# A decoder layer on one core: the same instructions, each engine's stages in another order

## The reference

```
# 1. attention, 16 heads of 8: q, k from a linear map joined with a 3-tap convolution; v linear
scores = einsum('bhqd,bhkd->bhqk', Q, K) / sqrt(8)
scores = scores * tau[..., None] + delta[:, :, None, :]   # tau, delta: conv, gelu, conv, sigmoid of x
out = linear(softmax(scores) @ V)
x = layernorm(x + out)
# 2. mLSTM, 4 heads of 32, q = x, k = v = ctx; ig, fg: gates, linear in q, k, v
log_D = cumsum(log_sigmoid(fg))[s] - cumsum(log_sigmoid(fg))[t] + ig[t]   # t <= s, else -inf
C = (q @ k.T / sqrt(32)) * exp(log_D - max_log_D)
h = C / (max(|C.sum(-1)|, exp(-max_log_D)) + eps) @ v;  x = layernorm(x + headnorm(h))
# 3. ffn: x and weight rounded to an FP6 grid in blocks of 32
x = layernorm(x + quantised(x) @ quantised(weight).T + bias)
```

## Time and profile before

| | us |
|---|---|
| median of 3 runs | 239.37 |
| the runs | 236.99, 239.37, 241.14 |
| the profiled execution | 238.0 |
| its span in the profile | 236.3 |
| PE busy | 208.4 (88%) |
| PE weight loads busy | 132.0 (56%) |
| DVE busy | 154.1 (65%) |
| ACT busy | 134.2 (57%) |
| POOL busy | 132.0 (56%) |
| mean granted clock of PE | 0.949 |

### The profile page before, as it was taken

How to read it: one execution, slowest core, us unless ns; L and a number is a source line. 1 busy time by engine, 2 the same in 40 slices (tenths; PEclk the granted TensorE clock), 3 DMA queues, 4 the chain that set the end, 5 groups by cost and what they waited for, 6 DMA issues and landing times. The chain is left out here.

```text
span 236.3 us, 5909 instructions
## 1 busy us (share of the span) xinstructions
PE 208.4 (88%) x2217; PEld 132.0 (56%) x2217; DVE 154.1 (65%) x354; ACT 134.2 (57%) x346; POOL 132.0 (56%) x239
## 2 busy tenths in 40 slices
PE   1799889699999999899888899789889969699895
PEld 1676454244566455566546567366648756276552
DVE  4587889959444553557647779966684475556871
ACT  2632867556854643673763768757776465515332
POOL 7994629691232192581695848862781757523520
PEclk9997999979999999999999999999997967899799
DMA  5822110000000000202002003003002003000001
GB/s 145 206 37 78 47 47 0 1 0 3 0 3 3 0 3 1 92 3 81 11 1 94 3 1 115 0 25 97 23 0 67 28 8 103 3 22 1 22 1 47
DMA packets 10220, 8.40 MB, mean 36 GB/s; under 512 B 1872, under 2 KB 9264, under 8 KB 10192
## 3 DMA queue, kind: packets, MB, share of 16 engines
q1 hardware_dynamic: 8816, 7.83, 11.2%
q0 software_dynamic: 512, 0.18, 0.7%
q10 hardware_dynamic: 864, 0.01, 0.2%
HBM read 6.94 MB, written 1.08 MB: 34 GB/s over the span
## 5 line engine op out<-in xcount | busy, mean ns | idle before, releaser
L996 DVE TENSOR_REDUCE nm<-score 128x8 f32<-128x1024 f32 x32 | 39.1, 1223 | 22.0 <-PE score L740 22.0
L511 ACT ACTIVATE prob<-score 128x1024 f32<-128x1024 f32 x32 | 32.6, 1021 | 21.2 <-PE score L755 21.0
L740 PE MATMUL score<-km,qf 32*128 32x512 f32 x128 | 35.0, 640 | 0.8 <-ACT prob L511 0.7
L750 PE MATMUL score<-qm,kf 32*128 32x512 f32 x128 | 35.0, 639 | 0.8 <-DVE nm L996 0.8
L775 PE MATMUL pvb<-ones 128*128 128x512 bf16 x80 | 23.5, 436 | 0.0
L359 POOL CAST nmx<-nm 128x16 bf16<-128x16 f32 x16 | 4.1, 254 | 30.4 <-DVE nm L996 30.4
L381 POOL TENSOR_TENSOR u<-u,maskb 128x1024 f32<-128x1024 f32 x7 | 16.5, 2358 | 7.2 <-DMA u<-gates_out 7.2
L768 PE MATMUL pvb<-prob,vz 128*32 128x128 f32 x512 | 17.4, 277 | 2.2 <-ACT prob L511 2.2
L859 PEld LDWEIGHTS qkb<-ctm,cc 128*128 128x128 f32 x128 | 15.3, 194 | 4.3 <-issue 2.2
L768 PE MATMUL pvb<-prob,ez 128*32 128x128 f32 x512 | 16.9, 273 | 0.0
L859 PE MATMUL qkb<-ctm,cc 128*128 128x33 f32 x128 | 15.7, 278 | 1.3 <-DVE cc L1069 0.8
(11 more groups left out here) (248 smaller groups left out, 485.8 us busy)
## 6 DMA issues: line engine op xcount, KB each, us to landing
u<-gates_out SPq DMA_DIRECT2D x7, 512.0 KB, 3.7
xt<-in_x_dram SPq DMA_DIRECT2D x4, 256.0 KB, 4.3
cin<-in_ctx_dram SPq DMA_DIRECT2D x4, 256.0 KB, 3.4
out_dram<-th SPq DMA_DIRECT2D x8, 128.0 KB, 1.9
ck<-in_L_attn_convk_w_dram SPq DMA_DIRECT2D x1, 192.0 KB, 3.6
cq<-in_L_attn_convq_w_dram SPq DMA_DIRECT2D x1, 192.0 KB, 3.9
pk<-in_L_attn_kproj_w_dram SPq DMA_DIRECT2D x1, 128.0 KB, 2.9
pq<-in_L_attn_qproj_w_dram SPq DMA_DIRECT2D x1, 128.0 KB, 3.4
```

The lines of the kernel that those rows point to most:

```text
L511: nc.scalar.activation(prob[:, n % 2, 2 * h:2 * h + 2, :].rearrange("p g s -> p (g s)"), sc[:, 1024 * h:1024 * (h + 1)], ACT.Exp, scale=0. ...
L740: ins = mm(sc[:, 512 * q:512 * (q + 1)], qf[r, n, :], km[r, n % (2 * CB)].rearrange("p j s -> p (j s)"), start=True, stop=True)
L750: mm(sc[:, 512 * q:512 * (q + 1)], kf[r, m, :], qm[r, m % (2 * CB)].rearrange("p j s -> p (j s)"), start=True, stop=False)
L996: nc.vector.tensor_reduce(nm[:, n % RING, 8 * h:8 * (h + 1)], sc[:, 1024 * h:1024 * (h + 1)].rearrange("p (h s) -> p h s", h=8), AX_X, ALU ...
```

## The change

The core of the diff, with the numbers of some stages:

```diff
-    "warm": (172, 173, 174, 177, 178, 180, 181, 184, 186, 188, 190, 191, 194, 196, 197, 198, 199, 200, 201, 204, 205, 206, 207, 208, 210, 211, 213, 214, 215, 216, 217, 218, 219, 220, 222, 223, 225, 226, 227, 228),
+    "warm": (172, 174, 175, 177, 178, 179, 180, 184, 187, 189, 190, 191, 195, 196, 197, 198, 199, 200, 201, 204, 205, 206, 207, 208, 210, 211, 212, 213, 215, 216, 217, 218, 219, 220, 221, 222, 224, 225, 227, 228),
-    "nGT": (73, 97, 102, 127, 148, 158, 170, 187), "qk": (83, 104, 114, 133, 157, 168, 189, 193),
-    "hst": (88, 108, 119, 142, 164, 175, 192, 203), "xdT": (116, 128, 135, 163, 179, 195, 209, 221),
+    "gT": (67, 80, 105, 120, 139, 154, 167, 186), "nGT": (71, 95, 107, 123, 149, 164, 170, 188),
+    "qk": (81, 108, 122, 131, 152, 169, 185, 193), "hst": (85, 114, 126, 141, 156, 173, 192, 203),
...
                 if due("x2l", t) is not None:
                     dve.wait_ge(rs2_done, LATE + 1)
                     dve.wait_ge(qa_done, LATE)
+                    dve.wait_ge(x2b_done, LATE)
```

More of the change, by code:

```diff
@@ L44 @@
 PLACES = {
[10 rows of a table removed]
-    "hst": (88, 108, 119, 142, 164, 175, 192, 203), "xdT": (116, 128, 135, 163, 179, 195, 209, 221),
-    "ffn": (117, 129, 137, 166, 182, 202, 212, 224),
-    "warm": (172, 173, 174, 177, 178, 180, 181, 184, 186, 188, 190, 191, 194, 196, 197, 198, 199, 200, 201, 204, 205, 206, 207, 208, 210, 211, 213, 214, 215, 216, 217, 218, 219, 220, 222, 223, 225, 226, 227, 228),
-    "vzero": (0,), "wab_o": (1,), "tapt": (2, 10, 15, 18, 24, 26, 33, 34), "wm_o": (3, 7),
-    "tapd": (4, 5, 17, 20, 27, 29, 36, 38), "ww_o": (6, 12), "wt_o": (8,), "wd": (9,), "fb": (11,), "bias": (13,),
@@ L60 @@
-    "ko": (14, 32, 56, 60), "wo_o": (16,), "qo": (19, 28, 35, 41), "wr_o": (21,), "qs": (22, 30, 39, 42),
-    "wg_o": (23,),
-    "max": (25, 31, 37, 40, 43, 45, 47, 48, 51, 53, 57, 59, 61, 63, 67, 69, 76, 79, 81, 84, 88, 95, 99, 106, 111, 113, 116, 126, 130, 132, 135, 140),
[7 rows of a table removed]
-    "x2l": (185,), "xdl": (187,), "outl": (189,), "xe": (0, 8, 9, 17), "idt": (1, 2, 12, 13, 24, 26, 37, 38),
-    "idd": (3, 4, 14, 19, 30, 31, 42, 46), "get": (5, 10, 16, 21, 28, 32, 41, 43),
-    "ged": (6, 7, 20, 23, 34, 35, 47, 49), "cxe": (11, 22, 48, 58), "th": (15, 25, 36, 50), "dt": (18, 29, 40, 52),
@@ L73 @@
-    "cme": (27, 33, 39, 45, 51, 56, 60, 63),
-    "nmTe": (44, 55, 62, 66, 73, 77, 82, 90, 99, 107, 118, 127, 140, 144, 152, 162), "edx": (53,),
-    "exps": (54, 57, 59, 61, 64, 67, 70, 72, 75, 76, 79, 83, 86, 91, 94, 98, 101, 105, 110, 113, 122, 124, 130, 135, 142, 145, 147, 151, 158, 160, 167, 168),
[6 rows of a table removed]
-    "mkk": (0, 1, 2, 3, 17, 18, 19, 23, 36, 37, 40, 41, 49, 51, 52, 53), "res": (4, 5, 6, 12),
-    "mkq": (7, 8, 10, 11, 14, 15, 20, 22, 38, 39, 42, 43, 57, 58, 59, 60), "gcb": (9, 13, 21, 24, 26, 27, 31, 32),
[3 rows of a table removed]
@@ L87 @@
-    "out": (75, 81, 85, 96, 102, 107, 110), "x2b": (109,), "spread": (0, 1, 2, 3, 6, 8, 9),
-    "store": (4, 5, 7, 10, 11, 12, 13, 14),
+    "spread": (0, 1, 2, 4, 6, 7, 9), "store": (3, 5, 8, 10, 11, 12, 13, 14),
+    "mkk": (3, 6, 7, 8, 16, 18, 19, 20, 33, 34, 36, 37, 50, 51, 53, 54),
+    "mkq": (9, 10, 12, 13, 21, 22, 23, 24, 40, 41, 42, 43, 59, 60, 61, 62), "res": (1, 2, 4, 11),
+    "ez": (28, 30, 38, 45, 49, 65, 70, 79), "gcb": (0, 5, 14, 17, 25, 27, 29, 32),
+    "split": (15, 26, 31, 35, 39, 44, 47, 52, 57, 64, 67, 72, 77, 82, 85, 91), "dma": (46, 55, 69, 76, 86, 92, 99),
@@ new lines @@
+    "dm": (48, 56, 71, 78, 87, 94, 100), "z2": (58, 73, 80, 88, 95, 101, 105), "x2": (63, 74, 83, 90, 96, 103, 106),
+    "x2b": (109,), "xd": (66, 75, 84, 93, 98, 104, 108), "out": (68, 81, 89, 97, 102, 107, 110), "xe": (0, 8, 11, 17),
+    "idt": (1, 2, 10, 12, 23, 24, 36, 37), "idd": (3, 4, 20, 21, 34, 35, 45, 48),
+    "get": (5, 9, 14, 16, 29, 31, 43, 47), "ged": (6, 7, 26, 27, 39, 41, 49, 50), "cxe": (15, 25, 40, 52),
+    "th": (13, 28, 38, 51), "cme": (18, 19, 30, 32, 46, 56, 59, 61), "dt": (22, 33, 44, 53), "edx": (54,),
@@ new lines @@
+    "nmTe": (42, 57, 63, 67, 71, 79, 87, 92, 102, 109, 115, 124, 136, 143, 154, 166),
+    "exps": (55, 58, 60, 62, 64, 66, 69, 73, 75, 77, 81, 85, 89, 91, 96, 99, 105, 107, 111, 117, 120, 123, 127, 130, 140, 144, 146, 150, 160, 162, 168, 169),
[11 rows of a table added]
+    "nmT": (30, 42, 51, 57, 62, 70, 82, 88, 94, 102, 112, 119, 130, 140, 148, 160),
[4 rows of a table added]
+    "xdT": (106, 132, 146, 163, 181, 194, 209, 223), "ffn": (111, 134, 150, 168, 182, 202, 214, 226),
+    "warm": (172, 174, 175, 177, 178, 179, 180, 184, 187, 189, 190, 191, 195, 196, 197, 198, 199, 200, 201, 204, 205, 206, 207, 208, 210, 211, 212, 213, 215, 216, 217, 218, 219, 220, 221, 222, 224, 225, 227, 228),
@@ new lines @@
+    "wab_o": (2,), "wt_o": (7,), "wm_o": (5, 13), "ww_o": (9, 15), "bias": (16,), "wd": (8,), "wo_o": (14,),
+    "wr_o": (17,), "wg_o": (32,), "fb": (10,), "vzero": (0,), "tapt": (1, 6, 11, 12, 23, 24, 34, 35),
+    "tapd": (3, 4, 21, 22, 31, 33, 39, 40), "ko": (18, 27, 41, 68), "qo": (19, 28, 36, 42), "qs": (20, 30, 38, 43),
+    "ed": (45,),
+    "max": (25, 26, 29, 37, 44, 46, 48, 49, 51, 53, 56, 59, 61, 65, 69, 73, 77, 79, 82, 86, 90, 94, 100, 103, 106, 113, 117, 124, 127, 131, 135, 144),
[8 rows of a table added]
```

## The result

The changed kernel takes 250.33 us (median of 4 runs, 248.58 to 251.34), beside 238.22 for the kernel before (median of 4, 236.99 to 241.14) on the same chip: a ratio of 1.058, 95% interval 1.051 to 1.064. The prediction was 236.0 us, so it is off by 14. Runs of one kernel spread by a few per cent, so every ratio in this text compares only the runs within 1.5% of each kernel's fastest, and needn't be the ratio of the medians. The profiled execution took 250.2 us, a span of 248.4, against 236.3 before.

What follows compares the result with a forecast made beforehand. PE bounds the bulk (busy 119.24 of 130.70 us), a chain of latencies the tail. 236.3 - 1.6 - 1.4 - 0.6 + 0.9 = 233.6, with 1.7 around it 235.3, moved half way towards the median: 236.0 us; range 231.0 to 241.0.

Steps and rivals of the forecast that it cites:

- The head's walk: Stretch up to the first scores: new order with old durations, `ph` 4 starting at 61.7 us against 61.99.
- The forecast's allowance for this: Head: if a stretch at 1.2 GHz falls on it, PE's lead is about 2.0 us instead of 3.7.
- The lead: PE ahead after the head by 3.4 us of early work: taken as 2.8 us, reduced to 1.0 at `y1` 7.
- The bulk's walk: From `ph` 4 to `y1` 7: PE idle time again about 11.5 us, `y1` 7 starting at 191.7.
- The waits that the text names: PE in the bulk: `ph` 18 waits about 0.8 us, `pv` 11 and `pv` 14 likewise, `pv` 15 about 1.0.
- The tail's terms: From `y1` 7 on: `F` 7 1.6 us earlier, `c` 6 gains 1.4, `c` 7 0.6, last part 0.9 later.
- the 1.4: Tail: gain in us for `c` 6, from `qk` 6 moving ahead of `gT` 7 and `nGT` 7; up to 1.9 possible.
- the 0.9 of the last part: End chain: `ffn` 6 behind four fillers instead of two, so L1140 waits for it and the end comes 0.9 us later.
- The slower rival: POOL's queue hangs behind `out` 0, ahead of `dma` 2, `dm` 2 and `split` 11: 244.3 us in all; chance 0.11.
- the 138 named as its point: Slower rival's threshold: `out` 0 on POOL decides the time if it ends later than 138 us.

Runs made afterwards that it cites:

- e3: Changed kernel with one PE step, `wt` 0, moved back behind `ww` 0: 247.54 us, ratio to the kernel before 1.054.
- e7: Kernel before with `wt` 0 right behind `wm` 0 on PE and `wab_o` 0 behind `tapt` 0 on DVE: 241.54 us, ratio 1.019.
- e15: Changed order up to `ph` 4, behind it the order of the kernel before, tail included: 244.49 us, ratio to before 1.018.
- e5: Changed kernel with eight short DVE steps of the bulk put ahead of the longer steps they stood behind: 243.31 us, ratio to before 1.025.
- e14: Kernel before with two short DVE steps, `scan` 3 and `scan` 4, put behind maxima 23 and 28: 245.16 us, ratio 1.028.
- e2: Kernel before with only the stretch behind `y1` 7 in the changed order: 237.80 us (10 runs) beside 238.38.

## Why the prediction was wrong

**The head's walk failed, "`ph` 4 at 61.7".** It started at 69.7. `wm` 0 came 1.8 us late as worked out (10.53). Not in the sum: that `wt` 0, moved past `wm` 1 and `ww` 0, waits for a load (0.94), with `wm` 1 and `ww` 0 behind it, and that `wt` 0 and `ta` 0 then stand in time at the low level (2.7 and 3.76 us), with durations taken from the old order, which had them at the high one (1.5 and 1.9). The forecast's allowance for this, 1.7 us less lead, was too small. e3 and e7 price the place of `wt` 0 at 2.8 to 4.3 us (e7 with `wab_o` 0 late as well) of a head that costs 4.3 to 5.7. The lead itself failed too: the 3.4 us of early work moved into idle time for which it was counted did not come out as a lead at `y1` 7 even with the old bulk (e15). The assumed lead of 2.8 was a loss.

**The bulk's walk failed, "about the 11.5 us of idle time again".** The waits that the text names came: `ph` 18 0.74, `pv` 11 and `pv` 14 0.75 each; `pv` 15 did not wait. The `F` 6 wait shrank from 1.37 to 0.35, as forecast. Missing were `att` 0 and 1, `F` 0, `gT` 1, `nGT` 2 and `hst` 3, 1.0 to 1.3 us each: I walked PE's order for cover and did not price the place of each short DVE step behind a maximum of 1.22 us. e5 puts this at 7.0 us with the low clock that goes with it. `y1` 7 was forecast at 191.7 and started at 207.0.

**The waits' second cost was not in the sum.** Two added waits of 2.7 us in all cost 6.3 by the medians (e14): 3.9 of the 8.3 us in its bulk are the low level, 1.7 a longer wait ahead of `F` 6. The walk used durations at the high level.

**The tail's terms held in sum.** Forecast from `y1` 7 to the end 41.9 (233.6 less 191.7), measured 41.4. DVE and POOL, the answers to the earlier trace rows:

```profile
210.78 2.24 DVE L1081 TENSOR_SCALAR hn<-hn 128x8 f32<-128x8 f32 x1
...
213.16 1.85 DVE L1020 TENSOR_TENSOR gb<-x,gcb 128x16 f32<-128x16 f32 x1
...
221.10 1.29 DVE L1061 SCALAR_TENSOR_TENSOR cc<-score,u 128x512 f32<-128x512 f32 x2
...
238.67 0.39 DVE L1140 TENSOR_TENSOR abT<-yb,x2b 128x256 f32<-128x256 f32 x1
```

```profile
210.62 2.36 POOL L380 TENSOR_TENSOR u<-u,maskb 128x1024 f32<-128x1024 f32 x1 [0.50 <-DMA u<-gates_out]
213.06 1.91 POOL L384 TENSOR_TENSOR u<-u,g 128x1024 f32<-128x1024 f32 x1
```

Two DVE steps were held by POOL's two, each to its end, as the text said. One thing differs: the step held first is L1081, which reads a single tile and two constants, and not L1083's counterpart L1082, which reads two operands and runs behind it. So a DVE step need not read two SBUF operands to be held. PE, the answers to the earlier trace rows:

```profile
208.04 0.59 PE L774 MATMUL pvb<-ones 128*128 128x512 bf16 x2
208.47 1.87 PE L858 MATMUL qkb<-ctm,cc 128*128 128x33 f32 x16
...
217.12 0.44 PE L818 MATMUL qkb<-lf,triu 128*128 128x8 f32 x2
```

`hst` 5 starts 0.3 behind the end of `y1` 7. `F` 7 comes 10.1 us behind the start of `y1` 7, forecast 10.2 (203.53 - 1.6 less 191.7), 10.8 before. `c` 6 starts 4.0 behind `F` 7, where 3.2 was forecast and 4.6 stood before: 0.6 of the 1.4. Against it the 0.9 of the last part was not paid: L1140 at 238.67 has no idle time in front. That the sum comes out within 0.5 is thus in part luck: one term too large and one that was not paid. As a gain of the whole, the tail by itself isn't shown (e2).

**The slower rival named the wrong queue.** POOL at `out` 0 (L422) and `dma` 2 (L380):

```profile
143.53 0.72 POOL L422 TENSOR_SCALAR th<-abT,rs 128x128 f32<-128x128 f32 x2 [3.42 <-ACT rs L439]
144.21 2.38 POOL L380 TENSOR_TENSOR u<-u,maskb 128x1024 f32<-128x1024 f32 x1
```

`out` 0 ended at 144.2, past the 138 named as its point, but in a bulk that was itself late: it ended as long after `scan` 2 (139.1, whose data `dma` 2 needs) as that transfer takes, about 5 us in the other pairs, so it held up little. The change does what it says only in part: the waits ahead of `F` 6, `gT` 6 and `nGT` 6, which make up the idle time of the earlier trace rows, fell to 0.35 us in sum (and 0.78 came ahead of `y1` 7), but over the bulk idle time grew by 4.3.
